# Eight expert loads moved from the head of one sync program to the end of the one before it

## The reference, cut to what matters

```python
scores = softmax(xf @ Wg)                     # 4096 tokens, 32 experts
weights, indices = top_k(scores, 4)
for e in range(32):
    tok = the tokens that chose expert e      # at most C = 2048
    out = (silu(xf[tok] @ W1[e]) * (xf[tok] @ W3[e])) @ W2[e] * w
    y = y.at[tok].add(out)
z = swiglu(xf, Ws1, Ws3, Ws2)                 # shared expert
return y + z
```

## Time and profile before

| what | us |
| --- | --- |
| median of 3 runs | 1339.29 (1336.46 to 1340.03) |
| the profiled execution's own time | 1338.2 |
| span of the profiled execution | 1336.5 |
| PE, busy in the span | 1172.4 (88%) |
| DVE, busy | 768.7 (58%) |
| ACT, busy | 521.4 (39%) |
| POOL, busy | 434.9 (33%) |

### The profile page before, as it was taken

The page is one execution under the profiler, slowest core; times in us unless marked ns, Lnnn a source line. Parts: engine busy times, 40 slices in busy tenths (PEclk is TensorE's granted clock), DMA queues, the critical chain, the costliest instruction groups (busy, mean ns, idle before and its releaser), DMA issues. The chain is left out here.

```text
span 1336.5 us, 27175 instructions
## 1 busy us (share of the span) xinstructions
PE 1172.4 (88%) x8528; PEld 811.5 (61%) x8528; DVE 768.7 (58%) x2032; ACT 521.4 (39%) x1049; POOL 434.9 (33%) x559
## 2 busy tenths in 40 slices
PE   7789999789867199999998177999989999999998
PEld 4367777555544088888886034878755455554554
DVE  4257777868764066667665693888872434334331
ACT  6545555333230035544543165565641222212221
POOL 5221111167777455565555262222110000000000
PEclk9889999978889599999999588999999999999999
DMA  8199100026247355555452840000000000000000
GB/s 181 25 310 388 55 1 2 25 84 120 92 164 268 131 170 162 158 169 170 151 158 59 340 170 13 2 1 1 2 0 1 16 17 17 1 16 16 16 16 16
DMA packets 100740, 123.77 MB, mean 93 GB/s; under 512 B 33984, under 2 KB 76051, under 8 KB 100631
## 3 DMA queue, kind: packets, MB, share of 16 engines
q1 hardware_dynamic: 86807, 87.98, 22.1%
q0 software_dynamic: 13824, 34.38, 7.2%
HBM read 61.78 MB, written 64.72 MB: 95 GB/s over the span
## 5 line engine op out<-in xcount | busy, mean ns | idle before, releaser
L1871 PE MATMUL psA<-H,B 128*128 128x512 f16 x1024 | 223.5, 379 | 0.0
L1798 DVE SCALAR_TENSOR_TENSOR H<-psA,H 128x512 f16<-128x512 f32 x128 | 88.3, 690 | 208.3 <-ACT H L1839 208.3
L1557 POOL DMA_INDIRECT y_rows<-YB,pair x160 | 155.5, 972 | 119.7 <-issue 62.3
L1839 ACT ACTIVATE H<-psA 128x512 f16<-128x512 f32 x128 | 76.4, 597 | 252.7 <-PE psA L1871 252.7
L1871 PEld LDWEIGHTS psA<-H,B 128*128 128x128 f16 x1024 | 100.0, 98 | 119.5
L1667 PE MATMUL psH<-W,XT 128*128 x640 | 166.1, 382 | 0.0
L1230 POOL DMA_INDIRECT x_rows<-XN,slot_s x128 | 130.8, 1022 | 51.0 <-issue 45.1
L871 ACT ACTIVATE PHT<-psT 128x512 f16<-128x512 f32 (+1 forms) x192 | 93.6, 521 | 121.1 <-PE psT L931 121.0
L812 DVE TENSOR_REDUCE mx<-psS 128x8 fp32r<-128x616 f32 x128 | 101.4, 794 | 51.7 <-PE psS L910 49.9
L819 DVE TENSOR_TENSOR PLT<-psT,PHT 128x512 f16<-128x512 f32 (+1 forms) x192 | 109.3, 596 | 24.0 <-ACT PHT L871 24.0
L1667 PEld LDWEIGHTS psH<-W,XT 128*128 128x128 f32 x640 | 110.1, 192 | 8.8 <-issue 0.3
(11 more groups left out here) (250 smaller groups left out, 2069.5 us busy)
## 6 DMA issues: line engine op xcount, KB each, us to landing
XG<-x_rows SPq DMA_DIRECT2D x160, 134.0 KB, 2.5
y_rows<-zero_row SPq DMA_DIRECT2D x4, 4096.0 KB, 27.3
G<-y_rows SPq DMA_DIRECT2D x7, 2048.0 KB, 10.2
x_rows<-zero_row SPq DMA_DIRECT2D x33, 134.0 KB, 2.9
X<-in_x SPq DMA_DIRECT2D x8, 512.0 KB, 7.1
QT<-in_w SPq DMA_DIRECT2D x1, 4096.0 KB, 17.6
out_x<-OUT SPq DMA_DIRECT2D x8, 512.0 KB, 2.9
y_rows<-YB,pair POOLq DMA_INDIRECT x160
```

The source lines that it names most:

```text
L1557: pool.indirect_dma_start(y_rows[:, :], bass.IndirectOffsetOnAxis(ap=pair[u // HALF][:, u % HALF:u % HALF + 1], axis=0), YB[u][:], None, b ...
L1798: dve.scalar_tensor_tensor(out=H[layer][1][:, o], in0=psA[k % 4][:], scalar=0.0, in1=H[layer][0][:, o], op0=ALU.max, op1=ALU.subtract).the ...
L1871: last = pe.matmul(psA[k % 4][:], W[:, c, o * P:(o + 1) * P], src[part][:, c], start=n == 0, stop=n == 2 * n_in - 1)
```

## The change

Three things are done. `XG`, its eight semaphores `gathered` and SP's eight registers are allocated before `route`, and the two row buffers `XN` of `route` become the two halves of `XG`. SP's program in `route` ends with waits for the finished plan and for all scatters, and then with `fetch_first`: the register load of the first eight first rows and the eight loads of tiles 0 to 7. `experts` starts its fetches at tile 8.

```diff
-    def route(norm, tail, counts, plan_all, own_f, next_w, load_down):
+    def route(norm, tail, counts, plan_all, own_f, next_w, load_down, XG, fetch_first):
...
-        XN = [space(st, "XN", [P, MT, ROW]) for _ in range(ROWBUFS)]
+        XN = [XG[:, b * MT:(b + 1) * MT, :] for b in range(ROWBUFS)]
...
+        plan_out_s = sem("plan_out")
...
                         sp.dma_start(x_rows[ds(row, P), :], zero_row[:, 0:ROW]).then_inc(tails_st, 16)
+                sp.wait_ge(plan_out_s, 1)
                 sp.wait_ge(tails_st, 16 * EXPERTS)
+                for b in range(ROWBUFS):
+                    sp.wait_ge(scattered[b], SCATTERS * len(range(b, MACROS, ROWBUFS)))
+                fetch_first(sp)
...
-                    dve.tensor_copy(plan_all[:], psR[:].rearrange("p (k j) -> p k j", k=2))
+                    dve.tensor_copy(plan_all[:], psR[:].rearrange("p (k j) -> p k j", k=2)).then_inc(plan_out_s, 1)
...
-    def experts(W13, W2, w_loaded, plan_all, own_f, binary):
+    def experts(W13, W2, w_loaded, plan_all, own_f, binary, XG, gathered, first_row):
...
-        XG = space(st, "XG", [P, AHEAD, ROW])
...
-                regs = [sp.alloc_register(f"first_row_{n}") for n in range(AHEAD)]
-
                 def fetch(j, u, g):
                     if u == 0:
-                        sp.reg_load(regs, plan_all[0:1, 1, j:j + AHEAD])
-                    row = sp.snap(regs[u], min_val=0, max_val=SLOTS)
-                    if g:
-                        sp.wait_ge(turned, j - AHEAD + 1)
-                        sp.wait_ge(met, 2 * g + u // HALF - 1)
+                        sp.reg_load(first_row, plan_all[0:1, 1, j:j + AHEAD])
+                    row = sp.snap(first_row[u], min_val=0, max_val=SLOTS)
+                    sp.wait_ge(turned, j - AHEAD + 1)
+                    sp.wait_ge(met, 2 * g + u // HALF - 1)
                     sp.dma_start(XG[:, u, :], x_rows[ds(row, P), :]).then_inc(gathered[u], 16)
 
-                for j in range(ETILES):
+                for j in range(AHEAD, ETILES):
...
+        def fetch_first(sp):
+            sp.reg_load(first_row, plan_all[0:1, 1, 0:AHEAD])
+            for u in range(AHEAD):
+                row = sp.snap(first_row[u], min_val=0, max_val=SLOTS)
+                sp.dma_start(XG[:, u, :], x_rows[ds(row, P), :]).then_inc(gathered[u], 16)
```

More of the change, by code:

```diff
@@ L1522, in experts @@
             "turned", "xt_out", "h_done", "silu", "h_out", "h_turned", "ht_out", "y_done", "y_out"))
-        gathered, stored = ([sem(s) for _ in range(AHEAD)] for s in ("gathered", "stored"))
+        stored = [sem("stored") for _ in range(AHEAD)]
         met, meta_own = (sem(s) for s in ("met", "meta_own"))
@@ L1945, in build @@
         retire()
-        route(norm, tail, counts, plan_all, own_f, layer1, load_down)
-        experts(W13, W2, (w_loaded, 16 * (2 * KC + 1)), plan_all, own_f, BinaryWeights())
+        loads = ExitStack()
+        XG = space(loads, "XG", [P, AHEAD, ROW])
+        gathered = [sem("gathered") for _ in range(AHEAD)]
+        first_row = [nc.sync.alloc_register(f"first_row_{n}") for n in range(AHEAD)]
+        def fetch_first(sp):
[3 more added lines that the diff above has]
+                sp.dma_start(XG[:, u, :], x_rows[ds(row, P), :]).then_inc(gathered[u], 16)
+        route(norm, tail, counts, plan_all, own_f, layer1, load_down, XG, fetch_first)
+        experts(W13, W2, (w_loaded, 16 * (2 * KC + 1)), plan_all, own_f, BinaryWeights(), XG, gathered, first_row)
+        loads.close()
         moe.close()
```

## The result

The changed kernel takes 1340.95 us, the median of 20 runs (1338.86 to 1343.88); the kernel before takes 1338.49, the median of 20 (1335.44 to 1341.95). The ratio is 1.0020, with a 95% interval of 1.0012 to 1.0028: slower by 2.5 us, clear of no change but within 0.3%. The forecast was 1341.3 us, and 2.0 us slower. The profiled execution of the changed kernel took 1342.81 us, with a span of 1341.1.

What follows compares the result with a forecast made beforehand. The prediction took PE's pace to bound `experts`, so its start moves the stage's end. Saving 1.9 us of landing and paying 3.8 us for eight issues gave +2.0 us on 1339.3: forecast 1341.3 us, range 1337.9 to 1345.2.

Steps and rivals of the forecast that it cites:

- The bound: In `experts`: PE sets the pace from first tile to last, so moving the first tile moves the stage's end equally.
- Buffers and waits: In `route`: sharing XG's halves and SP's waits for plan and scatters were to cost nothing.
- SP's steps: End of `route`: first load at about 459.6 us, then seven steps of 0.586 us, eighth issue over at 464.05.
- the least certain term: Time of one issue by SP at the end of `route`, taken as 0.586 us.
- the bounds of 0.36 and 1.27: Least and greatest time in us of one SP issue at the end of `route`, giving sums of +0.4 and +6.8.
- the second rival: SP's last stretch before the meeting: each issue costs 1.27 us, time 1346.1 us; chance 0.08.
- The meeting: End of `route`: SP comes after POOL, so the engines' meeting is over at 464.4 us, 3.8 us later.
- The third rival: End of `route`: SP's DRAIN waits until its loads have landed, +4.1 us, time 1343.4 us; chance 0.03.
- The first transpose: Start of PE in `experts`: 465.5 us against 463.56, 1.9 to 2.0 us later, with no wait for a load.
- The first rival: Border of `route` and `experts`: landing saved, meeting not late, PE starts at 461.7, time 1337.4 us; chance 0.06.
- The overlap rule: Advice to issue a DMA early and wait late; alone it would give back the landing's 1.9 us.
- The clock: Start of `experts`: PE's 4.14 us at half clock taken as unchanged, with bounds of 2.1 us gain or loss.

Runs made afterwards that it cites:

- e1: Changed kernel with shared buffers and added waits kept, but SP's register load and eight loads back at the head of `experts`: 1339.44 us, ratio 1.0005.
- e3: Changed kernel with eight more transfers of the same size issued by SP ahead of the eight early loads: 1345.32 us, ratio 1.0053.
- e4: Changed kernel with PE's first register load moved to the end of its program in `route`: 1338.50 us, ratio 1.0008.
- e2: Changed kernel with only the loads of tiles 0 and 1 early, six at the head of `experts`: 1337.30 us, ratio 0.9994.
- e6: Changed kernel with two early loads, SP's register load ahead of its waits and PE's in `route`, on a slower chip: 1385.23 us, ratio 1.0000.
- e10: The changed kernel again, on a chip where the kernel before took 1386.23 us: 1388.11 us, ratio 1.0029.
- e9: The kernel of e6 again, on a chip where the kernel before took 1386.23 us: 1386.38 us, ratio 0.9990.

## Why the prediction was right

*The bound.* `experts` runs at PE's pace from its first tile: the stall at tile 9 was 1.28 us again, and the handover carried through to the end of the stage. From the end of the scatters to the end of the stage's last meeting it was 737.1 - 458.9 = 278.2 us before and 738.5 - 457.6 = 280.9 after: 2.7 more, 1.8 of it the handover and 0.7 the time at half the clock.

*Buffers and waits cost nothing.* e1 shows it for the way to the first transpose. The plan would not have shown at the 13 us of lateness that the prediction gives: it was there at 422.6 in the kernel before, 13.8 us ahead of the last strip's issue, but after the strips SP waits for the scatters until 458.9 in any case.

*SP's steps.* The first load was expected 0.7 us behind the scatters and came at 0.7. Its price, the least certain term, was 0.586 a step. The seven steps took 462.1 - 458.3 = 3.8 us, 0.54 each: 0.3 us less than in the sum. The rows show where the sum had it from: in the earlier trace rows the last MOVE is at 465.1 and the last issue 0.4 us behind it, while after they are at 462.0 and 462.1. One slow step had gone into the mean of seven. e3 gives 0.56. Both are far from the bounds of 0.36 and 1.27, so the second rival, slow issues, is out.

*The meeting.* SP's DRAIN started at 5.2 (predicted: about 5.25), in part by luck: the issues were over 0.3 us early, at 462.4, and the way from there to the DRAIN took 0.4 us instead of 0.1. It took 0.126 us, with loads in flight; the eighth load had been issued 0.7 us before it and needs 2.1 at the least. The third rival, a DRAIN of SP that waits for landings, is out. The meeting was over 5.5 us after the scatters, the forecast being 464.4 - 458.9, just that.

*PE.* The first transpose came at 6.5, the forecast being 6.6. The 1.0 us for the register load is right in the changed kernel, and e4 shows that it is on the path. The first rival, the landing saved without a late meeting, would have shown a start at 2.8; it is out for eight loads. With two loads the landing is nearly all hidden (e2). The overlap rule of the Trainium skill, page "DMA: Bandwidth & Descriptors", section "Rules for kernel authors", is borne out for the landing itself, as the load did leave the path; what it leaves out is the issue time ahead of a meeting, here 3.8 us to hide 1.9.

*The clock.* Taken as unchanged, with bounds of 2.1 us either way. The profile had 0.7 us of loss from it, while in e2 the second product already took 1.03 us. The start at half the clock measured 1.3 us in one pair of profiles and 1.8 in another, against the 2.1 taken. Whether the clock has a share in the 2.5 us of the medians is open: single profiles can't tell it, as the kernel of e6 differed by 1.2 us in this term from one profile to another.

The measured 2.5 against the forecast 2.0 lies inside what the intervals allow (1.6 to 3.7 us). That the time itself, 1340.95 us, is so near the forecast 1341.3 is luck in part: with 20 runs the kernel before has a median 0.8 us lower than with the three it was forecast from, and the loss came out 0.5 us larger.

## What to carry to other kernels

A transfer's latency can be hidden ahead of a meeting of the engines, but each issue there that makes its engine the last to come is paid by every engine, so move only the loads that the first steps need: here two issues hid nearly all of the landing and eight cost twice what they hid. Before moving work ahead of a meeting, look up who comes last to it and by how much: SP had 21 us to spare, but none of it after POOL's last scatter, to which the change bound it; there it had 1.6 us, 0.7 of them for its registers. And take a handover's length from the event that releases it, since the whole time of one execution moves by more than the handover does.

## What the runs showed that was not expected

SP's issue of eight loads with addresses from registers took 4.11 to 4.16 us in every profile in which it stood at the end of `route`, on a chip with 1338 us and on one with 1386, while its 32 strips of zeros just ahead took 21.8 us on the first and between 29.9 (e10) and 44.6 (e9) on the other. The rows of the strips show part of how. L1213 and L1214 are the register step and the issue of a strip; first of the changed kernel's own profile, then of e9's:

```profile
L1213 SPq FUSED_REGOPS  x32: 44/44/64, 414.6 to 436.1; - x32
```

```profile
L1213 SPq FUSED_REGOPS  x32: 3/44/709, 448.5 to 492.8; - x32
...
L1214 SPq MOVE x_rows<-zero_row x32: 3/29/709, 448.6 to 492.9; - x32
```

The medians are the same, but the longest of these steps took 0.7 us in e9, where the longest register step of the first took 64 ns. What holds them up was not tried. The kernel before was 3.5 to 3.9% slower on the later chips (1385.7 to 1390.6 us) than on the first (1338.18). The order in which the engines reach a meeting is therefore not a property of the kernel alone.

Nor does the short DRAIN of SP hold for every engine. At the end of `experts` (L1533) POOL's took 6.6 us in the changed kernel, against 1.365 us at the end of `route`, where it had waited for its scatters first. Its last scatter was issued by 733.9, 2.2 us into this DRAIN, which ended at 738.3. Whether it waited for landings was not tried.

```profile
L1533 POOLq DRAIN  x1: 6617/6617/6617, 731.7 to 731.7; - x1
```
